# A causal second pass without mask matmuls: GpSimd writes the zeros, and the lanes' order is laid anew

## What is computed

```python
x = x + _L0_attn_ref(_layernorm(x), ...)     # scores over 512 tokens, only the diagonal of the softmax is kept
x = x + _L0_ffn_ref(_layernorm(x), ...)      # 2 layers of: 8 heads of 64, windows of 64 tokens, then a gated MLP
x = x + _L1_attn_ref(_layernorm(x), ...)     # 16 heads of 8, causal
x = x + _L1_ffn_ref(_layernorm(x), ...)      # 8 experts, two of them weighted in per token, and one shared expert
```

```python
score = jnp.einsum('bhnd,bhmd->bhnm', q, k) * scale
causal = jnp.tril(jnp.ones((S, S), dtype=bool))
score = jnp.where(causal, score, -jnp.inf)
attn = jax.nn.softmax(score, axis=-1)
out = jnp.einsum('bhnm,bhmd->bhnd', attn, v)
```

## Time and profile before

| | |
|---|---|
| median of 3 runs | 1685.44 us (1678.63 to 1690.98) |
| the profiled execution | 1693.07 us, its span from first to last instruction 1691.3 us |
| busy: PE, DVE, ACT, POOL | 1524.2, 1220.1, 967.2, 599.3 us |
| mean granted TensorE clock | 0.975 of full speed |

### The profile page before, as it was taken

One profiled execution on the slowest core, in us unless ns is written; L12 is line 12 of the kernel. 1 busy time (PEld: TensorE's weight loads), 2 busy tenths in 40 slices (PEclk: granted clock), 3 DMA queues, 4 the chain that ended last, 5 costly groups with the idle time before them and its releaser, 6 DMA issues. The chain is left out here.

```text
span 1691.3 us, 29695 instructions
## 1 busy us (share of the span) xinstructions
PE 1524.2 (90%) x11565; PEld 909.8 (54%) x11632; DVE 1220.1 (72%) x2636; ACT 967.2 (57%) x1787; POOL 599.3 (35%) x401
## 2 busy tenths in 40 slices
PE   5779987899989999998999989989998999988999
PEld 2454543546555555645556465655655546645556
DVE  6876878776679657886588856896669657876544
ACT  3475665467644866548744677447764553562551
POOL 1965737153161711707043350616207024110000
PEclk8999998999999999999999999999999999998999
DMA  4200001310151101600025100331016003413102
GB/s 143 68 2 22 23 8 29 70 24 2 39 128 29 24 1 47 148 3 23 10 76 110 25 2 28 97 71 24 1 47 141 3 1 86 102 35 80 42 20 60
DMA packets 37292, 80.13 MB, mean 47 GB/s; under 512 B 6782, under 2 KB 22654, under 8 KB 33776
## 3 DMA queue, kind: packets, MB, share of 16 engines
q1 hardware_dynamic: 37152, 78.22, 18.9%
HBM read 54.74 MB, written 8.78 MB: 38 GB/s over the span
## 5 line engine op out<-in xcount | busy, mean ns | idle before, releaser
L1507 POOL TENSOR_TENSOR fsmall<-fsmall,consts 128x8 f32<-128x8 f32 (+1 forms) x140 | 202.3, 1456 | 214.1 <-DVE fsmall L1133 208.8
L509 PE MATMUL ps<-bxt,mw 128*128 128x512 f32 x504 | 251.2, 608 | 4.1 <-DVE bigs L1479 3.5
L1528 POOL TENSOR_TENSOR work<-work 128x1024 f32<-128x1024 f32 x56 | 134.4, 2401 | 338.5 <-DVE work L1206 338.4
L509 PE MATMUL ps<-maskb,identb 128*128 128x128 bf16 (+1 forms) x1119 | 224.1, 237 | 30.5 <-ACT work L973 17.6
L973 ACT ACTIVATE work<-ps,fsmall 128x128 f32<-128x128 f32 x448 | 164.7, 507 | 50.7 <-DVE fsmall L1247 50.5
L1370 DVE TENSOR_REDUCE bsmall<-ps 128x1 f32<-128x512 f32 (+3 forms) x308 | 177.3, 631 | 13.2 <-PE ps L509 12.8
L1056 ACT ACTIVATE bigs<-ps 128x512 f32<-128x512 f32 x280 | 152.0, 646 | 32.7 <-PE ps L509 31.7
L1086 ACT ACTIVATE bigs<-ps 128x512 f32<-128x512 f32 x126 | 75.2, 598 | 155.0 <-PE ps L509 154.4
L509 PE MATMUL ps<-wqkv,h 128*128 128x512 f32 x336 | 158.3, 601 | 4.0 <-ACT vs L933 2.5
L1559 POOL TENSOR_TENSOR work<-work,fsmall 128x1024 f32<-128x1024 f32 x56 | 106.2, 1897 | 142.1 <-DVE fsmall L1238 142.0
L514 PE MATMUL ps<-ident,work 128*128 128x128 f32 x924 | 133.8, 285 | 23.5 <-ACT work L973 15.2
(11 more groups left out here) (337 smaller groups left out, 2975.0 us busy)
## 6 DMA issues: line engine op xcount, KB each, us to landing
mw<-in_experts SPq DMA_DIRECT2D x63, 384.0 KB, 3.2
pks<-scr_partsb SPq DMA_DIRECT2D x42, 192.0 KB
pqs<-scr_partsb SPq DMA_DIRECT2D x126, 64.0 KB
v2s<-vs SPq DMA_DIRECT2D x14, 512.0 KB, 4.4
v2s<-vs SPq DMA_DIRECT2D x14, 384.0 KB, 5.7
scr_partsb<-bigs SPq DMA_DIRECT2D x7, 768.0 KB, 3.7
wqkv<-in_experts SPq DMA_DIRECT2D x9, 384.0 KB, 3.2
out<-x SPq DMA_DIRECT2D x7, 256.0 KB, 8.9
```

The source lines that it names most:

```text
L509: return nc.tensor.matmul(o, a, b, start=start, stop=stop, skip_group_check=True)
L1507: return nc.gpsimd.tensor_tensor(out, x, consts[:, k:k + 1].broadcast_to([x.shape[0], x.shape[1]]), op)
L1528: nc.gpsimd.tensor_tensor(R.qk[:, m, :], R.qk[:, m, :], R.part[m % 2], ALU.add).then_inc(R.l_add.sem, 1)
```

## The change

The mask matmul in the second pass is gone, and with it the mask `causal_kq` (the other masks stay; the first pass is as it was). Behind each exp POOL now runs one `affine_select` in place on the first 128 columns of the fill's block, or of both blocks in one instruction (128x256 elements): it keeps an exponential where query >= key and writes zero elsewhere. It waits for that fill's exp (`c_e`) and counts on a new semaphore, `c_k`. PE's `pv{g}0` waits for the tenth count of `c_k` in place of `c_e`. The scores' own wait (`c_e`, a bank is free) is as before.

POOL so has 40 new steps in each sequence, `s{g}{n}.{r}`, and its string grows from 304 to 624 letters. The strings of all five engines are laid anew; those of PE, ACT and DVE have the same letters in number.

```diff
-        "BEBEBBBBFFFFFFFFBFFBFFFBBFBFBFBFBBBBBBEFFFFFFFFFFFFFFBFBFFBBBBBBBBBBBBBBBEFFFFFFFFFFBFFFFFFFFFFFFFFFFFFEFFF"
...
+        "BEBEBBBBBBFFFFFFFFFBFFFBBFBFBFFBFBBBBBBEFFFFFFFFFFFFFFFBBFBBBBBBBBBBBBBBBEFFFFFFFFFBFFFFFFFFBBBBBBBBBBFFBBBB"
+        "BBBBBBFFBFBBBBBBBBBFFFFFBFBBBFBBBBBBFFEFFFFBNEFFFFFEFFFFFFFFFFFBBBBBBBFBBBFFFBBBBFBBBBBBFFFFFBFBBBBBBBBBFFFF"
...
+        self.c_k = sig("c_future_cleared", 4 * 10)
...
-                            mm(bank[:, at:at + cols], R.pk[r][:, hh, kk * P:(kk + 1) * P], R.pq[r][:, hh, kk * P:T], stop=False)
-                            i = mm(bank[:, at:at + P], identb[:, :], causal_kq, start=False)
+                            i = mm(bank[:, at:at + cols], R.pk[r][:, hh, kk * P:(kk + 1) * P], R.pq[r][:, hh, kk * P:T])
...
-                                pe.wait_ge(R.c_e.sem, R.c_e.at(s, 10 * (gg + 1)))
+                                pe.wait_ge(R.c_k.sem, R.c_k.at(s, 10 * (gg + 1)))
...
+                def clear_future(gg, n):
+
+                    pool.wait_ge(R.c_e.sem, R.c_e.at(s, 10 * gg + n + 1))
+                    weights, blocks = R.big[n], len(EXP_FILLS[n])
+                    if blocks == 1:
+                        diagonal, pattern = weights[:, 0:P], [[1, P]]
+                    else:
+                        second = EXP_AT[EXP_FILLS[n][1]][1]
+                        diagonal = bass.AP(weights.tensor, weights.offset, [weights.ap[0], [second, 2], [1, P]])
+                        pattern = [[0, 2], [1, P]]
+                    nc.gpsimd.affine_select(diagonal, diagonal, pattern, ALU.is_ge, 0.0, base=0,
+                                            channel_multiplier=-1).then_inc(R.c_k.sem, 1)
+
+                for r in range(2):
+                    for g in range(2):
+                        for n in range(len(EXP_FILLS)):
+                            yield f"s{g}{n}.{r}"
+                            clear_future(2 * r + g, n)
```

More of the change, by code:

```diff
@@ new lines @@
+        "BFBBBFBBBBBFBBBFBBBBBBBBFBBFBFBBBBBFFBBFBBBBFBBBBBBBBBFBBFBBBBBBBFBBBBBBBFBFBBBBBBBBFBBFBBBBBBBBFBBFBFFBFFBB"
+        "FFBBBFFBBBBFBBBFBBFBFFFFFBFBBRBBEBFEBFEBFBBBBFBNEBBBEFFFEFFBEBNFEFBNBNBBEBFFFBBFBBFBFBBFBBBFBFBBFBFBFFFBBFBF"
+        "BFBBFBFBFBBBBBFFFBBFBBBFBBFFBBBBFBBFBBBFBBBFBBBBBBBBFBBFBBBBFBFBBFFBBBBFBBBBBFBBBFBBBFFBBBBBFBBBBFBBFFBBBFBB"
+        "BFBFBBBBBFBBBBFFFFBFBBBBFBBBBFBBFBFBBBFFBBBBFBBBBFEBFBEFFBEBBBFBBEFEBRBEBFFEBFBBENBBBFBNFBBFBBBBFBNBEBBFFFBN"
+        "FBFBBBFBBFBFBBBFBFFBBFFFBBBFFFBBFBFBBBBBFFBFFBBFBBBBFBFFBBBFFBBBBFBBFBBBBBBBFBFBBBBFFBBBBFFBBBBFBBBFBBBBBBFB"
@@ new lines @@
+        "BBBBFFBBBBBBBFBBBBBBBFBBBBFBBBBFFFBBFFBBFFFBBFFBBBBFBBBFBBBFBBFBBFFBBBBFBBBBFFEBFBFEFBERBBBEFEBBBEFFNEFBBBBB"
+        "FFBEBBBBNFBBBBFBENBFFFBBFBBNBFBFFBBBBFFBBBBBFFBBBFBFFBFFBFBFBFBBFBBFBFBBBFBFBBFBBFFBBBBFBBBFBBBFBBBFBBBBBBBB"
+        "FBFBBBFFBBFBFBBBBFBBBBBBFBBBFBBFFFBBBBBBFBBBBBFFFFBBBBBBBBBFBBFBFBBFBFBBFFBBBBBBFBBBBFFBBBFBFFBBBBFBBBEBFBFB"
+        "EFFBEBBFBRBBEFEBBNBNFEBBEFBFEBBFFFBBNFBNBFEBBFFBBFFBBBBFBFBBBBFBBFBBBBBFFBBFBFBBFFFFBBFFBBBBFBFBFBFFBFBBBBFF"
+        "BBBBFFBBFBBBBFBBBBBBBBBFBBBFBBBFBBBFFBBFBBBBFBBBBBBFBBBBFBFBBBBBBBFBBBFBBFBBFBBBBFBBBFFBBFBBFBFFFBBFBBBBBBBB"
@@ new lines @@
+        "FBBBBBBFFBBBBFBBBBFBFBFFFEFBEFBREFBBFBBNFBEBBNBBFEBNBFEFBEBBBNEFBBBBBFBBBBBFBBBFBEBBFFBBBFBBFBFBBBFBBBFFBBFF"
+        "FBBFBFBBFBBFFBBBBFBBBFBFBFBBBBFBBBBFBBFBBFBBBFBBFBBBBFBBBBFBBBFBBBBBBBFBBBBFBBBBBBBBBBBBBBFFBBBBBBBFBBBBBBBF"
+        "BBBBBBBBBBBBBBBBBBFBBBBFBBFFBFBRBBFBFBFBFBBBBNBFBNBFBBBBNBBBBBFFBBBBNBBBBBBFBFBBFBFBFBFBBBFBBBFBBBBBBBBFBFBB"
+        "FFFBFBBFFBBBBBFBBFBBBBFBBFBBBBBBBBBFFBBBFBBFFBFBBBBFBBBBBBBFBBBBBBBBBFBFBBBBBFBBFBBBBBBBBBBBBBBBBBBBBBBBBBBB"
+        "BBBBBBBBBFBFBFFBFFFFBFFRBFFFBFFFBBBBFFFFBFBBFFFBFBFFFBFBFFBFFBFFBFFFFBFBFBFFFBFBFFFFBFFFBFFFBFBFFFFFFBBFFFFF"
@@ new lines @@
+        "BBBBBBFFBFBBBBBBBBBFFFFBFBBBFBBBBBBFFEFFFFBNEFFFFFEFFFFFFFFFFFFBBBBBBBFBBBFFFBBBBFBBBBBBFFFFFBFBBBBBBBBBFFFF"
+        "BBFBBBBBBBBFBNEFFFFFFFFFFFFFFFFFBBBBBFBBBBBFFFBBBBBBBBBBFFFFFBBBBFBBBBFBBFFFFEBBFBBBBBBBBFBNEFFEFFFFFFFFFFFF"
+        "FFFBBBBBBBBFFBBFFFBFBBBBBBBBBFFFBBBBBFBBBBFBFFFFBFBBBBBBBBBFBNEFFFFFFFFFFFFFFFFFBBBBBBBBFBBFFBBBFBBBBBFBBFFF"
+        "BBFBBFBBBBBBFFBBBBFFBBBBBBFEFFBNEFFFFFFFFFFFFFFFFFBBBBBBBBBBBBBBBBBBBBBBBBBBBBBBBBBBBBBBBBBNFFFFFFFFFFFFFFFF"
+        "FBBBBBBBBBBFBBBBBBBBBBBBBBBBBBBBBBBBBBBBBBBFFFFFFFFFFFFFFFFFFFFFFFFFFFFFFFFFFFFFFFFF"
@@ L381, in program @@
         mean_w = sb("mean_w", [P, P])
-        maskb = sb("maskb", [P, 2 * T + 2 * P], BF16)
+        maskb = sb("maskb", [P, 2 * T + P], BF16)
         iota = sb("iota", [P, EXPERTS])
@@ L386, in program @@
         local_mask = [maskb[:, 0:T], maskb[:, T:2 * T]]
-        causal_qk, causal_kq = maskb[:, 2 * T:2 * T + P], maskb[:, 2 * T + P:2 * T + 2 * P]
+        causal_qk = maskb[:, 2 * T:2 * T + P]
         x2 = sb("x2", [P, 3, NT, P])
@@ L1721, in masks @@
     q, k = np.arange(P)[:, None], np.arange(P)[None, :]
-    kept = np.concatenate([first] * 4 + [keep] * 4 + [k <= q, q <= k], 1)
+    kept = np.concatenate([first] * 4 + [keep] * 4 + [k <= q], 1)
     return np.where(kept, 0.0, NEG).astype(np.float32)
```

79 lines of the change are left out of this document (31 added, 48 removed).

## The result

| | before | changed |
|---|---|---|
| median, us | 1685.86 (1678.63 to 1690.98, 4 runs) | 1735.21 (1733.06 to 1737.15, 4 runs) |
| ratio | | 1.0294, 95% interval 1.0262 to 1.0327 |
| profiled span, us | 1691.3 | 1732.4 |

The changed kernel is slower by 2.9%, 49 us in the medians and 41.1 in the spans of the two profiled executions. The forecast was 1689.8 with a range up to 1714: wrong, and outside the range. Slower by over 1% had 0.30.

What follows compares the result with a forecast made beforehand. PE was taken to set about two thirds of a shared pass, ACT the last third. -11.7 + 6.4 + 5.8 + 3.9 = +4.4 us on 1685.4 gave 1689.8 us; range 1664 to 1714, the sum's own 1672 to 1702.

Steps and rivals of the forecast that it cites:

- The masks: 512 mask matmuls taken off PE in the second passes, 28.2 us in all: -11.7 us, bounds -17.6 and -8.
- shared passes: Five second passes run beside another lane's work: masks 17.6 us gross, two thirds real; POOL's queue adds +5.8 us.
- bare passes: Three second passes paced by ACT and the handing over: 10.6 us of masks worth nothing, selects add +6.4 us.
- The selects' price: Time of one select on POOL: 0.32 us for one block, 0.48 for two, midway between memset and broadcast product.
- the third rival: A select is far dearer than its elements, 1 us each: about 1873 us; chance 0.05.
- The selects' cost: Time added by selects: +6.4 us in bare passes, +5.8 in shared ones as half of POOL's 2.3 us excess a pass.
- the ring: A bare pass's repeating group of ten exps, products with v and a copy: 7.98 us, about 8.5 with selects.
- twelve such groups: Groups in the bare passes where nothing covers the last select: 12 x 0.53 = +6.4 us.
- The order: New strings of all engines: six more ACT table loads, +3.9 us (bounds 0 and 7.7); everything else costed at nothing.
- The first (masks' time back whole): All 28.2 us of masks come back and selects cost only 4.3: 1661.5 us; chance 0.20.
- The second: POOL becomes the bound of the shared passes: 1712.6 us, or 1732 if no excess is covered; chance 0.25.
- Its second sign: Sign for POOL as bound of the shared passes: PE's waits for POOL reach 10 us and more in all.

Runs made afterwards that it cites:

- new_order_bare: The changed kernel with the selects taken off POOL and nothing in their place: new order, no masks, no selects; 1723.6 us, ratio 1.0218.
- old_order_new_passes: The kernel before, masks kept, with the new order only in the second passes of sequences 1 to 4; 1710.0 us, ratio 1.0139.
- new_order_masks: The kernel before with the new order on all engines, masks still added by PE, no selects; 1721.8 us, ratio 1.0210.

## Why the prediction was wrong

**What bounds the kernel: the failed reading.** "PE is the engine to relieve" came from busy shares. PE's 17.89 of 18.00 us hold the tails of matmuls, behind which waits disappear, and "what is taken from PE there comes back whole" didn't hold: the masks came back with 2.4 us (at most 5.7 by the interval) or nothing.

**The masks: -11.7 forecast, -2.4 to +1.8 measured.** The price of a mask was right (0.055 from start to start, and 0.54 against 0.44 for two fills). That two thirds of it are real in the shared passes was wrong; doubling the masks cost 6.4 of 28 us. The argument that had PE hidden in the bare passes holds for most of the shared ones too.

**The selects' price: right.** 0.303 and 0.410 us, undisturbed 0.29 and 0.41; 0.32 and 0.48 were forecast. They lie nearer to the memset's end of the bounds. The Trainium skill's rule for one input ("GPSIMD Engine Reference", section "Engine selection") says the same, and the trace agrees: 107 ns for 128 more columns is 0.84 ns each, the memset's slope. Its price for branching on the data did not apply: a select of one block took 0.30 us, not the estimate's 1.3, and with that the third rival fell.

**The selects' cost: the sum agrees, in part by luck, +12.2 forecast, +11.6 between the medians of `new_order_bare` and the changed kernel.** In the shared passes first to last exp is 262.8 us against 256.0, +6.8 (5.8 forecast); in the bare ones 103.0 against 100.3, +2.7 (6.4 forecast). The handing over in the ring was right: products to products is 8.45 us in sequence 5, where a bare step was 7.98 in sequence 6 before, and here is the wait of PE for the last select that makes it up (in the second row the products stand behind a matmul of the other lane, in the third they don't):

```profile
1386.63 2.36 PE L513 MATMUL ps<-bigs,vas 128*32 128x512 f32 x32
...
1395.08 2.36 PE L513 MATMUL ps<-bigs,vas 128*32 128x512 f32 x32 [0.69 <-POOL bigs L1601]
...
1403.53 1.06 PE L513 MATMUL ps<-bigs,vas 128*32 128x512 f32 x7 [1.55 <-POOL bigs L1601]
```

In sequence 6, for which 8.5 was forecast, the steps are 10.67, 8.45 and 10.14 us, where they were 9.81, 7.98 and 7.97. The last of them has a term that I lacked, the granted clock behind the wait (third row):

```profile
1539.97 2.36 PE L513 MATMUL ps<-bigs,vas 128*32 128x512 f32 x32 [1.55 <-POOL bigs L1601]
1550.64 2.36 PE L513 MATMUL ps<-bigs,vas 128*32 128x512 f32 x32 [1.25 <-POOL bigs L1601]
1559.09 4.05 PE L513 MATMUL ps<-bigs,vas 128*32 128x512 f32 x32 [1.55 <-POOL bigs L1601]
1569.23 4.00 PE L513 MATMUL ps<-bigs,vas 128*32 128x512 f32 x32 [1.55 <-POOL bigs L1601]
```

The products there take 4.05 us in place of 2.36. What was too much is the count of twelve such groups: in some, the new order has work of the other lane in front of the products. But that the cost falls away whole at 0.20 to 0.22 us a select, and hardly at all at 0.25 to 0.30, is in none of my terms; the clock fits it, no run tests it. In the shared passes the sum began from a misread length: 41.0 and 46.2 us run from the end of the table load, while from the first exp it is 40.0 and 43.0, and 45.3 in the mean of the five, not 47.9. By the prediction's own count POOL would then be 4.9 us too long in a pass, not 2.3, and its half +12 us, not +5.8. That +6.8 was measured near it is luck.

**The order: +3.9 forecast, +36 measured. This is the step that failed.** The count of table loads was right (136, and 9 in place of 7 from sequence 7's first exp on). The sentence behind it was not: "Everything else about the order I cost at nothing, since most of the steps stand within a few places of where they stood." A few places are enough. One step three, six and thirteen places earlier on PE (in sequence 3 with the window before it) costs 9 us with what follows from it, and one two places later on POOL is worth 10. I compared the strings for table changes and for what stands around the selects, and never for which step each engine would wait at. `sm2.1` in front of the products could be seen in the new string: the bank it needs is freed by ACT's local exps, and that a step of the F lane waits for ACT L973 was in the list of waits of before.

That step costs 9 us when it is put into the old order, but nothing came back when it was taken out of the new one, so it can't be booked as a share of the 36. The 36 us are spread over many small waits and aren't traced step by step; which placements make them stays open. The runs place the loss in the stretch from first exp to first expert, and show that it doesn't divide into stretches.

**The rivals.** The first (masks' time back whole) was wrong for the reason above. The second named slower, and 1732 for its worst case is near the 1735 that came, but for another reason: POOL is at 79 to 86% in the passes, and kernels with the new order and no select at all are at 1722 and 1724. Its second sign, PE's waits for POOL of over 10 us, did show (15.3 us for selects): a sign that a lesser cause gives too is no proof. That the order itself could be the cost was no rival, and had no chance or price. Nor does the sum's own range, 1672 to 1702, follow from the terms: with all of them at their upper bounds (-8, +15, +40, +7.7) it reaches 1740.

**Signs.** The table loads, the mask's records (x512 of 128 columns) and the select's duration came as forecast, the ring's step in sequence 6 only once in three. Of PE's waits for selects several were over the 1 us foreseen, up to 3.0.

## What to carry to other kernels

Before work taken off PE is counted as time, take the steps from start to start in that stretch and add them up against the pass: a high busy share of PE is no proof that PE sets the time. Where the order of in-order queues is laid anew, the order is a change of its own and wants its own term and its own rival: for each step that moved in front of another lane's, name the bank or tile it waits for and who frees it. And run the parts apart, new order with old work and old order with new work, before any part is credited or blamed. Read the granted clock behind each new wait of PE too: it can take back what shorter work gave.

## What the runs showed of the hardware

- A select of GpSimd (128 partitions, f32, in place) takes 0.20 us for 16 columns, 0.25 for 64, 0.30 for 128 and 0.41 for 256: a base of some 0.2 us, and 0.84 ns a column from 128 to 256.
- A stretch of this program can keep its length in other surroundings: the old order's passes of sequences 1, 3 and 4 took 49.6, 43.9 and 43.0 us in the new order's program, and 49.6, 44.0 and 43.0 in the old one's. That of sequence 2 did not (51.3 and 49.8); its granted clock was 0.97 in the one and 1.00 in the other.
- A wait of PE can cost more than itself. In `old_order_new_passes`, behind the wait of 2.86 us, the granted clock was 0.50 of full speed (1.2 GHz in place of 2.4), and the local scores took 1.99 us in place of 1.10; it was 0.50 again from 804 us on, behind 8 us in which PE was busy for 5.40. In the changed kernel's sequence 6 the products with v took 4.05 and 4.00 us in place of 2.36 behind two waits of 1.55 us, and 2.36 behind one of 1.55 and one of 1.25. Windows of `old_order_new_passes` (the clock is the third number from the end):

```profile
787.00:791.00 4.00, 1.16 (x33) 1.00 (x34) 2.33 (x5) 3.88 (x11) 3.13 (x2) 0.90 0.00 0
791.00:793.50 2.50, 2.48 (x33) 1.59 (x33) 0.95 (x2) 2.29 (x7) 1.43 (x1) 0.50 0.02 7
793.50:796.00 2.50, 2.39 (x36) 1.02 (x34) 2.18 (x3) 0.75 (x3) 0.46 (x1) 0.98 0.00 0
796.00:804.00 8.00, 5.40 (x67) 3.96 (x68) 6.80 (x12) 8.00 (x22) 4.97 (x4) 0.99 0.01 2
804.00:807.00 3.00, 3.00 (x39) 2.30 (x37) 1.61 (x3) 2.29 (x5) 1.83 (x1) 0.50 0.00 0
```

  Over the whole program it does not explain the order's cost: the mean clock is 0.975 before and 0.978 in `new_order_masks` (span 1719.8 us). What it can explain is smaller: from first exp to first SiLU the changed kernel has 37.1 us at 0.50 and `new_order_masks` 15.9, at most 10.6 us of time.
